# Carrying the routing gate with the scattered row, in a mixture-of-experts layer

## The reference

```python
scores = softmax(xt @ Wr)                    # 8 experts
topk_w, topk_idx = top_k(scores, 2)
topk_w = topk_w / (topk_w.sum(-1) + 1e-20)   # the two gates of a token
g = silu(einsum('th,ehd->etd', xt, Wg))      # 128 -> 256
u = einsum('th,ehd->etd', xt, Wu)
out_all = einsum('etd,edh->eth', g * u, Wd)  # 256 -> 128
...
```

## Time and profile before

| | |
|---|---|
| median of 3 runs | 3225.33 us (3221.89 to 3227.55) |
| span of the profiled execution, first to last instruction | 3058.8 us |
| median less the span: what lies around it | 166.5 us |
| TensorE products | 2564.5 us busy (84% of the span) |
| vector engine | 2019.8 us busy (66%) |
| ScalarE | 1803.4 us busy (59%) |
| GpSimd | 853.6 us busy (28%) |

### The profile page before, as it was taken

The page is one execution under the profiler, slowest core; times in us unless marked ns, Lnnn a source line. Parts: engine busy times, 40 slices in busy tenths (PEclk is TensorE's granted clock), DMA queues, the critical chain, the costliest instruction groups (busy, mean ns, idle before and its releaser), DMA issues.

```text
span 3058.8 us, 77303 instructions
## 1 busy us (share of the span) xinstructions
PE 2564.5 (84%) x26192; PEld 2090.3 (68%) x26193; DVE 2019.8 (66%) x5025; ACT 1803.4 (59%) x4422; POOL 853.6 (28%) x1042
## 2 busy tenths in 40 slices
PE   3899898989898998897997189999999987988990
PEld 2777777777777777776886166666766765776880
DVE  2677676767666776786665656666676666875664
ACT  2777777777777777563554155555556554654550
POOL 0000000000000000575566233424233224774660
PEclk9999999999999999776999598998999986768995
DMA  5221111112111210111322300000000000112225
GB/s 147 49 49 44 44 43 44 43 46 51 44 43 44 51 47 20 53 45 54 82 81 75 96 2 2 2 2 2 2 2 2 2 2 22 45 54 72 82 78 168
DMA packets 139323, 140.27 MB, mean 46 GB/s; under 512 B 30540, under 2 KB 105425, under 8 KB 138864
## 3 DMA queue, kind: packets, MB, share of 16 engines
q1 hardware_dynamic: 122096, 101.67, 13.2%
q0 software_dynamic: 16896, 34.12, 3.3%
HBM read 45.85 MB, written 40.54 MB: 28 GB/s over the span
## 4 chain that ended last, share of the span: by engine, by line
PE 55%; DVE 16%; issue 9%; ACT 9%; SPq 5%; DMA 4%; DVEq 1%; POOL 1%; ACTq 0%; POOLq 0%
PE psum L457 5%; PE psum L426 5%; PE psum L492 4%; SPq L412 3%; DVE state L1717 3%; PE psum L1514 3%; ACT probs L446 3%; PE psum L1137 3%; PE psum L1111 2%; DVE neg_max L435 2%; PE psum L1112 2%; PE psum L1562 2%; PE psum L1113 2%; DMA y<-y_tok 2%; PE psum L543 2%
## 5 line engine op out<-in xcount | busy, mean ns | idle before, releaser
L446 ACT ACTIVATE probs<-psum,neg_max 128x512 f32<-128x512 f32 (+3 forms) x1024 | 539.5, 538 | 244.7 <-DVE neg_max L435 242.6
L435 DVE TENSOR_REDUCE neg_max<-psum 128x1 f32<-128x512 f32 (+3 forms) x1024 | 457.3, 483 | 54.8 <-PE psum L427 25.8
L426 PE MATMUL psum<-ls,qs 96*128 96x512 f32 (+3 forms) x1024 | 383.6, 400 | 115.1 <-ACT probs L446 103.5
L457 PE MATMUL psum<-ident,probs 128*128 128x128 f32 x2560 | 431.4, 284 | 2.8 <-ACT probs L446 0.8
L324 POOL TENSOR_TENSOR rstd<-var_eps,half_neg 128x4 f32<-128x4 f32 x32 | 40.5, 1267 | 1115.3 <-DVE var_eps L320 1115.3
L426 PEld LDWEIGHTS psum<-ls,qs 96*128 96x128 f32 x1024 | 199.9, 195 | 219.2 <-ACT probs L446 164.3
L476 DVE COPY probs_t<-psum 128x512 f32<-128x512 f32 (+1 forms) x384 | 230.3, 600 | 147.5 <-PE psum L457 140.5
L1250 POOL DMA_INDIRECT y_tok<-yb,xb x272 | 267.3, 983 | 207.7 <-issue 116.9
L457 PEld LDWEIGHTS psum<-ident,probs 128*128 128x128 f32 x2560 | 275.9, 145 | 25.8 <-ACT probs_t L472 9.7
L914 POOL DMA_INDIRECT x_slot<-pay,pos_i x256 | 255.9, 1000 | 92.4 <-issue 77.2
L427 PE MATMUL psum<-causal_r,ident_r 128*128 128x128 f32 x1024 | 236.8, 244 | 0.0
(11 more groups left out here) (320 smaller groups left out, 6638.8 us busy)
## 6 DMA issues: line engine op xcount, KB each, us to landing
qs<-q_h SPq DMA_DIRECT2D x512, 64.0 KB, 2.0
xb<-x_slot SPq DMA_DIRECT2D x272, 66.0 KB, 1.8
qs<-q_l SPq DMA_DIRECT2D x256, 64.0 KB, 2.0
y<-y_tok SPq DMA_DIRECT2D x32, 512.0 KB, 3.8
y_tok<-yb,xb POOLq DMA_INDIRECT x272
x_sb<-in_x SPq DMA_DIRECT2D x16, 256.0 KB, 5.5
x_slot<-pay,pos_i POOLq DMA_INDIRECT x256, 2.3
out<-x_sb SPq DMA_DIRECT2D x16, 256.0 KB, 3.0
```

The lines of the kernel that those rows point to most:

```text
L426: pe.matmul(o[:, at:at + n], q, ls[par][0:3 * LD, 0:n], start=(at == 0), stop=False, skip_group_check=True)
L435: last = dve.tensor_reduce(neg_max[:, par, h, qt:qt + 1], bank[u % 3][:, at:at + (qt + 1) * P], AX.X, ALU.max, negate=True)
L446: last = act.activation(probs[:, u % 3, c], bank[u % 3][:, c], ACT.Exp, bias=neg_max[:, par, h, qt:qt + 1], accum_out=row_sum[:, par, h, q ...
L457: last = pe.transpose(bank[3 + u % 2][:, c:c + P], probs[:, u % 3, c:c + P], ident[:, :])
```

## The change

The gate is no longer kept in a tile of its own. `gates_vector` writes it to `pay[slot]`, in column 129 of the row, beside the row's number. The scatter takes it along to `x_slot`, and the expert stage's load brings it back in `xb`. There `gated_up` multiplies silu, up and the gate, in one instruction for each block of the pair, with the gate as a scalar for each partition. The down product then gives the output times its gate, so that combining is two plain additions of a whole sequence. The scatter has to wait for the gates (`gated`) in place of the positions (`pos_done`).

```diff
-        gates = sb("gates", [P, SEQS * QT, TOPK])
...
-        def gates_vector(dve, f, b):
+        def gates_vector(dve, f, b, slot):
...
-            dve.tensor_tensor(gates[:, bass.ds(b * QT, QT), :].rearrange("p t k -> p k t"), gate2[:, :, :],
+            dve.tensor_tensor(pay[slot][:, :, :, D + 1].rearrange("p t k -> p k t"), gate2[:, :, :],
...
         def scatter_gpsimd(pool, f, b, slot):
             z = fs
-            pool.wait_ge(z["pos_done"], f * SEQS + b + 1)
+            pool.wait_ge(z["gated"], f * SEQS + b + 1)
...
-            def gated_up(p, par):
+            def gated_up(p, par, j):
...
-                dve.tensor_tensor(bh[par][:, :, :], psum[:, 2 * par:2 * par + 2, F:2 * F], bs[par][:, :, :],
-                                  ALU.mult).then_inc(z["gu_mul"], 1)
+                for k in range(2):
+                    last = dve.scalar_tensor_tensor(out=bh[par][:, k, :], in0=bank[2 * par + k][:, F:2 * F],
+                                                    scalar=xb[:, j, k, D + 1:D + 2], in1=bs[par][:, k, :],
+                                                    op0=ALU.mult, op1=ALU.mult)
+                last.then_inc(z["gu_mul"], 1)
...
                 for k in range(TOPK):
                     if k:
                         dve.wait_ge(z["mixed_a"], f * SEQS + b + 1)
-                    for t in range(QT):
-                        xt = tile_x(b * QT + t)
-                        gate = gates[:, bass.ds(b * QT + t, 1), k:k + 1].rearrange("p o k -> p (o k)")
-                        last = dve.scalar_tensor_tensor(out=xt, in0=y2[par][:, t, k, :], scalar=gate, in1=xt,
-                                                        op0=ALU.mult, op1=ALU.add)
-                    last.then_inc(z["mixed" if k else "mixed_a"], 1)
+                    xv = x_sb[:, bass.ds(b * QT, QT), :]
+                    dve.tensor_tensor(xv, y2[par][:, :, k, :], xv, ALU.add).then_inc(z["mixed" if k else "mixed_a"], 1)
```

More of the change, by code:

```diff
@@ L1232, in body @@
                 if in_range(st):
-                    gated_up(st, j % 2)
+                    gated_up(st, j % 2, j)
                 if in_range(st - 1):
@@ L1352, in batch @@
                 place_vector(dve, f, b, slot)
-                gates_vector(dve, f, b)
+                gates_vector(dve, f, b, slot)
                 if has_before(b):
```

## The result

The change made the kernel slower. Its 20 runs have a median of 3244.35 us (3223.93 to 3259.95), against 3228.81 us for 20 runs of the kernel before taken beside them; the ratio is 1.0039, with a 95% interval of 1.0020 to 1.0057. The prediction was 3210.6 us, 0.5% faster.

A forecast was written before the change was run, and what follows sets the result against it. It took load-then-mix loops to bound combining, TensorE the expert stage, and TensorE and the vector engine in turns routing. Saving 7.3 + 8.5 - 1.1 = 14.7 us took 3225.3 to 3210.6 us, eight-in-ten range 3202 to 3219.

The forecast's parts named there:

- Routing, "Cost: 0": Routing: scatters start up to 1.3 us later, but 3.8 us of cover before the reader of rstd makes it free.
- 1.3 us a sequence over 32 sequences would be 42 us: Routing: the price of the later scatters if the cover were gone.
- Slower, by routing: Rival in routing: later scatters hold up the vector engine once 2.5 us later than thought; 3236 us at 0.8 us; chance 0.04.
- What bounds the kernel: Whole kernel: span 3058.8 us, the other 166.5 us unchanged; load-mix loops bound combining, TensorE the expert stage.
- Combining: Both combine stages: two adds replace eight pieces, mixes and loops shorten, saving 7.3 us in the second and 8.5 in the first.
- Contention: Rival in combining: loads closer together land later and eat the gain, about 3219 us; chance 0.12.
- Expert stage: Expert stage: two products take 0.80 us for 0.60 a pair, mostly covered; cost 1.1 us, bounds 0 and 4.
- 0.05 us at each of 14 such places: Expert stage, where the loop of eight pairs restarts: allowance for a later xt_l, 0.7 us in all.
- The sum: Whole kernel: 7.3 + 8.5 - 1.1 = 14.7 us saved, giving 3210.6 us, 0.5% faster.

The follow-up runs named there:

- e8: The change as it is, run once more on a chip where the kernel before took 3070.81 us: ratio to before 1.0010 (0.9989 to 1.0031).
- e1: The kernel before with only the scatter's wait moved from the positions to the gates: ratio to before 1.0096, 31 us more.
- e13: The change with the gates computed before the positions and the scatter waiting for both: 3212.49 us, ratio to the kernel before 0.9961.
- e15: The kernel before with a second power on GpSimd's queue ahead of each rstd, into a tile nobody reads: ratio to before 1.0005.
- e16: The kernel before with the power of rstd moved between the sixth and seventh scatter of a sequence: ratio to before 0.9947, 17 us less.
- e0: The kernel before, unchanged, run once more: ratio to before 0.9975 (0.9944 to 1.0006), where before took 3236.69 us.
- e3: The kernel before with only combining made two plain additions, gates computed but not applied: ratio to before 0.9941, 19 us less.

## Why the prediction was wrong, step by step

**The step that failed: Routing, "Cost: 0".** It took the cover from the reader of `rstd` (3.8 us) and from GpSimd's turn (11.5 us under 11.9). The first is right in the profile that it read; the second was thin, since half of the turns there last 11.7 us or less, but on kind B it held (median turns of 11.7 us before and of 11.6 and 11.7 in e8). On kind A what stands behind the scatters isn't `rstd` but `pos`, through a signal of TensorE that comes through 1.40 to 1.49 us after the row of scatters in the turns shown. There is no cover at all, and most turns grow by the 1.2 to 1.3 us of the gates. The working had the price ("1.3 us a sequence over 32 sequences would be 42 us"); the run of e1 gave 31 us for the wait alone, and the profile of the change 29.1 us in routing. The rival "Slower, by routing" was the right place, but it was to decide only once a scatter was 2.5 us later than thought; in the loop the first tenth counts. That the loop exists and that the scatters are in it is shown by e1, e13, e15 and e16. How the signal is held is not. That kind B was in the profile and kind A in the times was bad luck; that the working followed only the reader of `rstd` behind the scatters was not.

**What bounds the kernel.** The first step already had the sign of it: a span 166.5 us below the time, taken as work around the span. It was another kind of chip, with another limit in routing (turns of 11.1 to 12.7 us, but for the last sequences, against 13.5) and in the expert stage (steps of 2.95 us against 3.3 to 3.7 in the median).

**Combining: right, and somewhat small.** A mix of 1.53 us was counted and 1.42 came, for two additions of 0.69 us with 0.04 us between them in place of the 0.15 us; loops of 5.77 to 5.87 us were counted, and 5.60 came. Up to mix 3 of the first stage, beside GpSimd, 3.7 us were counted and 3.2 came (18.3 us in e0, 15.1 us in the change); behind it 4.8 were counted and 6.8 came. Counted in all 7.3 + 8.5 = 15.8 us; the stages show 19.0 us and the run of e3 19 us. Contention didn't show: the loads of the chain land in 3.84 to 3.89 us, before 3.78 and 3.90.

**Expert stage.** The price of the two products, 0.80 us for 0.60, was right. On kind B the steps inside the loop hide it (2.95 us in both). There the term "0.05 us at each of 14 such places" is the mis-sized one: a seam that keeps its clock costs 0.18 us more (8.03 against 7.85), and at most seams the fall of the clock adds 1.4 to 1.6 us; together 13 to 17 us in place of 1.1. The profile that the prediction read had none of the falls that the five others with one product show at 11 of 60 seams, and a fall of the clock stands nowhere in the working. That the added time comes of the product alone is argued from the seams of the traces and not shown by a run, since the product alone never ran on kind B. On kind A it shows no cost.

**The sum.** Kind A: -19 for combining, +31 for the wait, -6 for the products (each with some 10 us of uncertainty) make +6 us; measured +12.6 us (6 to 18). Kind B: -20 for combining, +13 to +17 in the expert stages, +2.5 in routing (186.4 + 186.7 - 185.4 - 185.2) make -4.5 to -0.5 us; measured +3 us (-3 to +10).

**A better version.** Gates first beats the kernel before on kind A by 0.39%, and equals it on kind B (0.9975 and 1.0000). The kernel before with the power after six scatters gains 0.53% on kind A, and 0.29 and -0.06% on kind B. Both together weren't tried.

## What to carry to other kernels

Compare a profile's span with the times it is to explain before anything else: here a gap of 5% meant that the trace and the times came from different machines or states, and the cover read from the one didn't hold in the other. Before something is added to a wait, follow the circle, not only the next reader: who, two steps on, starts by this instruction's end? Work that is ready before a wait belongs ahead of it; the order of six instructions of 0.2 us was worth some 25 us here. And a saving on one engine can be spent by a pause on another: look at TensorE's granted clock wherever its pause grows, by even 0.2 us.

## What was not expected of the hardware

- On three of five chips a semaphore that TensorE raises behind matmuls with records ending at 1325.88 was seen by the vector engine only at 1330.55, 1.46 us after GpSimd's eight indirect DMAs in a row ended (gaps of 0.30 us between them); a gap of 2.04 us in the row let it through. Over the 196 such waits of more than 1.2 us in ten profiles of kind A (all but e16) the median of that time behind the row is 1.41 us, and nine in ten lie between 0.8 and 1.6. On the other two chips `pos` was never waited for.
- TensorE's other signals come late there as well. The waits of e0 for something without a record (in total us, times, longest us):

```profile
DVE pos L894 <- remote: 64.0, 28, 3.9
ACT y_half L1188 <- remote: 45.4, 33, 2.9
ACT ht_h L1182 <- remote: 40.9, 27, 3.0
```

  `ht_h` and `y_half` belong to the expert stage, and ScalarE waits in both for TensorE. In e0 these waits end 0.76 us (`ht_h`) and 1.02 us (`y_half`) in the median after the end of a scatter to `y_tok`. All eleven profiles of kind A have such waits, and the nine of kind B have none at all. So late signals behind indirect DMAs mark the two kinds, in both stages. What differs between the chips is open.
- The two kinds of chip differ by 150 us on the same kernel (3071 and 3075 against 3213 to 3237), most of it where GpSimd issues indirect DMAs beside TensorE: between e0 and the profile of the prediction, 23 + 22 us in routing and 51 + 50 us in the expert stages, of 168 us in the span (3226.6 - 3058.8).
- Pauses of TensorE of 1.57 to 1.82 us at the seams were followed by some 3 us at a granted clock of 0.50 (1.2 GHz) at 25 of 36 seams; pauses mostly of 1.39 to 1.49 us at 11 of 72.
